# Latent attention loop: two scores by key ahead of the value products, and the fourth score by key of a step moved into the next step

## The chip, the cores and the metric

One core of one Trainium2 chip runs the whole program in one launch. The metric is the device time in microseconds (us). The program is a stack of four layers, each a cross attention and a feed-forward block, over 4 batches of 512 tokens of width 128. The change touches only the loop of the latent attention in the third layer, which takes some 210 us of the 1221 us.

## The reference, cut to what matters

Within the third layer's feed-forward block stands a latent attention (`_mla`): keys and values come from a latent of width 64, there are 16 heads of width 8, and a causal mask.

```python
def _mla(h, Wq, Wdkv, Wuk, Wuv, Wo):
    q = (h @ Wq).reshape(B, S, HEADS, hd)
    c = h @ Wdkv
    k = (c @ Wuk).reshape(B, S, HEADS, hd)
    v = (c @ Wuv).reshape(B, S, HEADS, hd)
    scores = jnp.einsum('bqhd,bkhd->bhqk', q, k) / jnp.sqrt(jnp.asarray(hd, h.dtype))
    causal = jnp.tril(jnp.ones((S, S), bool))
    scores = jnp.where(causal, scores, jnp.asarray(-1000000000.0, h.dtype))
    a = jax.nn.softmax(scores, axis=-1)
    out = jnp.einsum('bhqk,bkhd->bqhd', a, v).reshape(B, S, D)
    return out @ Wo
```

## The kernel before

Every engine runs its own hand-written program; semaphores tie them together. The latent attention is one loop over steps k = -8 to 75 (`STEPS`). A step stands for one head, and there are 64 heads in all (4 batches of 16), in 16 groups of four (a group is n, a head of it g). Each score matrix is made twice:

- `score(step, way)`, L933: scores by query, 512, 384, 256 and 128 columns for way 0 to 3 (causal). VectorE takes the largest of each row (`largest`, L2049). It runs `LEAD` = 8 steps ahead, so step k issues the scores of head k + 8.
- `score_by_key(step, j)`, L945: the transposed scores with the row maximum folded in, 512, 384, 256 and 128 columns for j = 0 to 3. ScalarE takes their exponent out of PSUM (`exponent`, L1309).
- `weigh(n, j)`, L961: eight fp32 matmuls (rows of the trace) with 32 stationary columns, probabilities times values, 512, 384, 256 or 128 columns. It runs `LAG` = 5 steps behind; so the 512-column one falls on k = 1, 5, 9, ..., the 128-column one on k = 4, 8, 12, ....
- `beside(name, n)`, the extras, at most one a step (`extra(k)`): projections of the next batch ("values" L907 at k = 10, 26, 42; "keys" L902 at 12, 28; "queries" L904 at 14, 30), "turn" L912 at every k = 1, 5, 9, ..., which transposes the row maxima of a group, and the way out ("out" L916 at 7, 15, 23, ..., "mix" L919 at 8, 24, 40, 56, "write" L922 at 11, 27, 43, 59). For k below 0 they are "values", "keys" and "queries" of batch 1 and the turn of group 0. They share PSUM bank 7, so each waits until the one before is read.

Scores by query share three PSUM banks, and scores by key three others (`RINGS` = 3), so each of the two kinds waits for the reader of the tile three before:

```python
wait(pe, qk_max, t - RINGS + 1)   # in score
wait(pe, kq_exp, t - RINGS + 1)   # in score_by_key, t = 4 * step + j
```

By this, `score_by_key(k, 3)` waits for the exponent of `(k, 0)`, `(k, 0)` for that of `(k - 1, 1)`, `(k, 1)` for that of `(k - 1, 2)` and `(k, 2)` for that of `(k - 1, 3)`. The probabilities have two sets of buffers (by n % 2). So on ScalarE the first exponent of a group carries one more wait, for a value product:

```python
if g == 0 and j == 0:
    wait(act, pv_ps, n - 1)
```

The value products of group n - 2 end with the one at step k = 4n, so that wait is for the `weigh` of the very step in which the exponent stands.

GpSimd masks the diagonal of each head's probabilities (`hide_later_keys`, L1534, waits for all four exponents of the head; `weigh` waits for it), splits the maxima of a group in pieces (`split_max`, L1512 to L1518, ahead of its turn) and, after ScalarE has copied the turn (L1298), spreads the result into the queries (`spread`, L1527), for which `score_by_key(4n, 0)` waits. SyncE brings the operands of each group by 18 DMAs (`stack`, L497); those of group n wait until the scores by key of group n - 4 are all done, and are first used by `score(4n, 0)`, at step 4n - 8. After groups 3, 7 and 11 it also spills the next batch (L486), and the next group's loads wait for the spill.

Of the kernel before, what the change touches and what calls it, by code (L numbers as in the profile page):

```python
# [20 lines left out]
TB = S // P  # L21
# [73 lines left out]
def extra(k):  # L95

    for name, every, offset, first, count in (("keys", 16, -20, 1, B), ("queries", 16, -18, 1, B), ("values", 16, -6, 0, B),
                                              ("turn", 4, -3, 0, QUADS), ("out", 8, 15, 0, UNITS),
                                              ("mix", 16, 24, 0, B), ("write", 16, 27, 0, B)):
        n, rest = divmod(k - offset, every)  # L100
        if rest == 0 and first <= n < count:
            return name, n
    return None
# [76 lines left out]
def build(nc, x_in, packed, w_ffn1, w_moe, w_mla, split2, w_ffn3, rope, mask1, mask3, normed1, sums1, out):  # L180
    ctx = ExitStack()
    with ctx:
# [341 lines left out]
        def _(pe):  # L524
# [366 lines left out]
            def beside(name, n):  # L891


                if (name, n) != EXTRAS[0]:
                    last = EXTRAS[NTH[name, n] - 1]
                    pe.wait_ge(extra_read, read(*last))
                    if last[0] == "write":
                        pe.wait_ge(x_new, XNEW0[MLA] + last[1] + 1)
                bank = ps[:, 7, :]
                block_of = lambda i: slice(i * P, (i + 1) * P)  # L900
                if name == "keys":
                    t = mm(bank, w_uk, c_s[0:LAT, cols(n)], start=True, stop=True)  # L902
                elif name == "queries":
                    t = mm(bank, w_q, FT[:, cols(n)], start=True, stop=True)  # L904
                elif name == "values":
                    for i in range(TB):
                        t = mm(bank[:, block_of(i)], c_s[0:LAT, n * S + i * P:n * S + (i + 1) * P], w("mwuv", LAT),  # L907
                               start=True, stop=True)
                elif name == "turn":
                    pe.wait_ge(nm_split, n + 1)  # L910
                    for i in range(TB):
                        t = mm(ps[SIGNS:P, 7, block_of(i)], nm_pieces[:, n % 2, i, :], identb[:, :], start=True, stop=True)  # L912
                elif name == "out":
                    pe.wait_ge(oT_sb, n + 1)
                    for i in range(TB):
                        t = pe.transpose(bank[:, block_of(i)], oT[:, block_of(i)], ident)  # L916
                elif name == "mix":
                    for i in range(TB):
                        t = pe.transpose(bank[:, block_of(i)], o_s[:, n * TB + i, :], ident)  # L919
                else:  # L920
                    for i in range(TB):
                        t = mm(bank[:, block_of(i)], oT_s[:, block_of(i)], w("mwo"), start=True, stop=True)  # L922
                t.then_inc(extra_ps, 1)
# [12 lines left out]
            def score_by_key(step, j):  # L936


                n, g = divmod(step, WAYS)
                t = WAYS * step + j  # L940
                if g == 0 and j == 0:
                    pe.wait_ge(neg_set, n + 1)
                wait(pe, kq_exp, t - RINGS + 1)
                rows = SIGNS + PIECES * WAYS
                mm(ps[:, 2 * (t % RINGS) + 1, 0:S - j * P], keys[0:rows, n % HOLD, g, j * P:(j + 1) * P],  # L945
                   queries[0:rows, n % HOLD, g, j * P:S], start=True, stop=True).then_inc(kq_ps, 1)
# [18 lines left out]
                    t.then_inc(pv_ps, 1)  # L965

            for k in STEPS:
                if extra(k) is not None:
                    beside(*extra(k))
                ahead, now = 0 <= k + LEAD < TB * QUADS, 0 <= k < TB * QUADS  # L970
                if ahead:
                    score(k + LEAD, 0)
                    score(k + LEAD, 1)
                if 0 <= k - LAG < TB * QUADS:
                    weigh(*divmod(k - LAG, TB))
                if now:
                    score_by_key(k, 0)
                if ahead:
                    score(k + LEAD, 2)
                if now:  # L980
                    score_by_key(k, 1)
                if ahead:
                    score(k + LEAD, 3)
                if now:
                    score_by_key(k, 2)
                    score_by_key(k, 3)

            prepare(MOE, lambda b: route(MOE, b, w("mgw")))
            pe.wait_ge(ld["moe"], 16)
# [57 lines left out]
        def _(act):  # L1047
# [264 lines left out]
            for k in STEPS:  # L1312
                if k >= 13 and (k - 13) % 8 == 0 and (k - 13) // 8 < UNITS:
                    u = (k - 13) // 8
                    act.wait_ge(pv_ps, 2 * u + 2)
                    if u >= 1:
                        act.wait_ge(extra_ps, put("out", u - 1))
                    go(oT, ps[:, 6, :], ACT.Copy).then_inc(oT_sb, 1)
                if extra(k) is not None:
                    beside(*extra(k))  # L1320
                if 0 <= k < TB * QUADS:
                    for j in range(TB):
                        exponent(k, j)

            starts(act, MOE)
            for b in range(B):
# [975 lines left out]
```

## Time and profile before

| | |
|---|---|
| median of 3 runs | 1234.56 us (1230.53 to 1235.0) |
| the profiled execution | 1222.78 us |
| its span | 1221.0 us |
| mean granted TensorE clock of the span | 0.892 |
| TensorE matmuls busy | 1003.9 us (82%) |
| VectorE, ScalarE, GpSimd busy | 830.3, 519.1, 485.9 us |

The profiled execution was 0.95% faster than the median of the other runs. In a view in order of time, a row has the start in us, the duration in us (of the whole merged run of instructions where "x2" or more stands behind), the engine, the line, the operation, output <- inputs and their size, and in brackets how long the engine sat idle before and what ended that. The durations of matmuls overlap, since they are pipelined: what a matmul costs TensorE is the distance to the start of the next. PE is TensorE, DVE VectorE, ACT ScalarE, POOL GpSimd, SPq SyncE's queue. In a view of busy time by stretch, a row has the stretch, its length, the busy us (and instructions) of matmuls, weight loads, VectorE, ScalarE and GpSimd, the granted clock, the DMA share and GB/s. The granted clock is that of TensorE, 1.00 being the 2.4 GHz level and 0.50 the 1.2 GHz level.

### The profile page before, as it was taken

Reading aid. Unit: us, or ns where it says so; the run is one execution under the profiler, and the core shown is the slowest. Engines: PE = TensorE matmul, PEld = TensorE weight load, DVE = VectorE, ACT = ScalarE, POOL = GpSimd, SP = SyncE. Lnnn points to the kernel's source line nnn. Section 1 sums busy time; section 2 is a strip of 40 time slices with the busy share of each in tenths; the row PEclk is TensorE's granted clock in tenths of the full one; section 3 lists DMA queues with packets and bytes.
Section 4 is the critical chain, followed back from the end, with each engine's and each line's share of the span. In section 5 each row is a group of like instructions: output and inputs, shape, how many; then the busy total and the mean of one; then the engine's idle time right before and its main releaser. Section 6 shows DMA issues by size and latency. Waiting matters only on the chain.

```text
span 1221.0 us, 20581 instructions
## 1 busy us (share of the span) xinstructions
PE 1003.9 (82%) x6807; PEld 720.7 (59%) x6811; DVE 830.3 (68%) x2125; ACT 519.1 (43%) x1266; POOL 485.9 (40%) x433
## 2 busy tenths in 40 slices
PE   4798795677776999967998698888889999569977
PEld 2577633556666899845776233333356777347774
DVE  4599488499966777578998366666423333778972
ACT  2455251244422555653442246665622333135532
POOL 3244254255514666213556666564530000314430
PEclk8899796589977999988999669999977999789998
DMA  8200000000011111220000222221020000000001
GB/s 307 98 1 1 1 1 0 1 1 1 1 36 26 45 42 45 85 74 1 0 1 1 82 67 64 70 77 50 11 87 1 0 0 0 1 1 1 1 1 35
DMA packets 22964, 40.21 MB, mean 33 GB/s; under 512 B 6272, under 2 KB 17792, under 8 KB 22240
## 3 DMA queue, kind: packets, MB, share of 16 engines
q1 hardware_dynamic: 20384, 33.99, 8.6%
q0 software_dynamic: 2496, 5.16, 1.6%
q8 instruction: 46, 0.75, 0.3%
q14 instruction: 38, 0.31, 0.1%
HBM read 31.31 MB, written 7.82 MB: 32 GB/s over the span
## 4 chain that ended last, share of the span: by engine, by line
PE 49%; issue 20%; DVE 15%; POOL 9%; ACT 5%; DMA 1%; SPq 1%; DVEq 0%; POOLq 0%; ACTq 0%
PE ps L800 6%; PE ps L716 5%; PE ps L752 5%; PE ps L742 4%; POOL att L1406 4%; PE ps L961 3%; PE ps L812 3%; DVE mx L1676 3%; PE ps L945 3%; PE ps L933 2%; DVE rs L1690 2%; PE ps L699 2%; PE ps L682 2%; PE ps L534 1%; PE ps L573 1%
## 5 line engine op out<-in xcount | busy, mean ns | idle before, releaser
L1406 POOL TENSOR_TENSOR att<-att,ri 128x1232 f32<-128x1232 f32 x64 | 177.5, 2773 | 221.1 <-DVE ri L1696 221.1
L716 PE MATMUL ps<-VW,PT 128*128 128x128 f32 (+3 forms) x1280 | 159.5, 280 | 29.5 <-DVE x L1708 27.8
L716 PEld LDWEIGHTS ps<-VW,PT 128*128 128x128 f32 (+1 forms) x1280 | 150.0, 193 | 48.8 <-DVE x L1708 44.4
L1139 ACT ACTIVATE PT<-ps 128x512 f32<-128x512 f32 x128 | 69.9, 595 | 129.1 <-PE ps L699 129.1
L2049 DVE CUSTOM_DVE_ANT_0 C<-ps,cmaskb 128x512 bf16<-128x512 f32 (+1 forms) x128 | 71.2, 557 | 70.9 <-PE ps L933 65.9
L1131 ACT ACTIVATE att<-att 128x1232 f32<-128x1232 f32 x64 | 79.0, 1234 | 51.6 <-DVE att L1683 51.5
L699 PE MATMUL ps<-W,att 128*128 128x128 f32 (+1 forms) x640 | 85.0, 282 | 12.0 <-POOL att L1406 12.0
L1690 DVE TENSOR_REDUCE rs<-att 128x16 f32<-128x1232 f32 x64 | 91.2, 1425 | 0.0
L1805 DVE SCALAR_TENSOR_TENSOR U<-ps,w_c,U 128x128 f32 x128 | 36.0, 344 | 77.8 <-PE ps L752 77.8
L752 PEld LDWEIGHTS ps<-U,att 128*128 128x128 f32 x512 | 68.2, 196 | 33.6 <-issue 31.4
L800 PE MATMUL ps<-PT,att 128*128 128x128 f32 x624 | 81.1, 285 | 4.3 <-issue 2.8
L945 PE MATMUL ps<-U,W 108*128 108x512 bf16 (+3 forms) x256 | 71.8, 327 | 15.0 <-ACT VW L1309 5.7
L933 PE MATMUL ps<-W,U 72*128 72x512 bf16 (+3 forms) x256 | 73.6, 337 | 12.7 <-DMA W<-split 8.1
L699 PEld LDWEIGHTS ps<-W,att 128*128 128x128 f32 (+1 forms) x640 | 72.7, 143 | 16.0 <-POOL att L1406 12.6
L800 PEld LDWEIGHTS ps<-PT,att 128*128 128x128 f32 x624 | 76.2, 199 | 7.0 <-issue 3.6
L945 PEld LDWEIGHTS ps<-U,W 108*128 108x128 bf16 x256 | 25.6, 102 | 78.5 <-issue 28.9
L752 PE MATMUL ps<-U,att 128*128 128x128 f32 x512 | 69.2, 281 | 2.5 <-ACT att L1168 2.5
L1373 POOL TENSOR_TENSOR rstd<-ve,minus_half 128x4 f32<-128x4 f32 x42 | 42.7, 1032 | 68.2 <-DVE ve L1585 54.7
L1383 POOL TENSOR_TENSOR VBD<-PT,W 128x1232 f32<-128x1232 f32 x6 | 13.5, 2252 | 141.5 <-issue 130.2
L1168 ACT ACTIVATE att<-ps 128x512 f32<-128x512 f32 x64 | 38.1, 597 | 70.5 <-PE ps L742 70.5
L742 PE MATMUL ps<-FT,U 128*128 x128 | 67.6, 616 | 0.0
L1676 DVE TENSOR_REDUCE mx<-ps 128x16 f32<-128x1232 f32 x32 | 46.0, 1438 | 27.8 <-issue 12.3
(332 smaller groups left out, 2225.4 us busy)
## 6 DMA issues: line engine op xcount, KB each, us to landing
U<-in_ffn SPq DMA_DIRECT2D x1, 6176.0 KB, 23.5
U<-split SPq DMA_DIRECT2D x144, 32.0 KB
W<-split SPq DMA_DIRECT2D x144, 32.0 KB
W<-in_packed SPq DMA_DIRECT2D x1, 2162.5 KB, 22.4
U<-in_ffn SPq DMA_DIRECT2D x1, 2060.0 KB, 8.1
U<-in_moe SPq DMA_DIRECT2D x1, 2048.0 KB, 8.4
split<-VBD SPq DMA_DIRECT2D x4, 384.0 KB, 3.0
split<-W SPq DMA_DIRECT2D x4, 384.0 KB, 2.7
```

Of the source, the lines that this page charges most:

```text
L699: q = pe.transpose(ps[0:m, (3 if s == X2 else 4) + k, (c % 4) * P:(c % 4 + 1) * P], att[:, 2 + t.slot(2), c * P:c * P + m], ident)
L716: q = mm(attended(s, t), PT[0:m, t.slot(2), c, :], batch(VW, t.group)[0:m, c * D:(c + 1) * D], start=(c == 0), stop=(c == NC - 1))
L742: mm(ps[:, u % 2, :], W1M[:, e, j * P:(j + 1) * P], FT[:, cols(c)], start=True, stop=True)\
L752: t = mm(ps[:, 4 + e % 2, i * D:(i + 1) * D], hh[:, u % 2, i * P:(i + 1) * P], W2M[:, e, j, :], start=(j == 0 and i == 0), stop=(j == J2 - ...
L800: t = mm(ps[:, 2 + 2 * k + a, c * P:(c + 1) * P], chosen1[:, k, at:at + P], pickedT[:, k, :], start=True, stop=True)
L933: mm(ps[:, 2 * (t % RINGS), 0:(i + 1) * P], queries[0:STACK, n % HOLD, g, i * P:(i + 1) * P], keys[0:STACK, n % HOLD, g, 0:(i + 1) * P], s ...
L945: mm(ps[:, 2 * (t % RINGS) + 1, 0:S - j * P], keys[0:rows, n % HOLD, g, j * P:(j + 1) * P], queries[0:rows, n % HOLD, g, j * P:S], start=T ...
L1131: go(att[:, 2 + t.slot(2), :], att[:, t.slot(2), :], ACT.Exp, scale=scale).then_inc(expd, 1)
L1406: tt(p, p, over_keys(ri[:, t.slot(2), :]), ALU.mult).then_inc(probs, 1)
L1676: v.tensor_reduce(top, src, AX.X, ALU.max).then_inc(rowmax, 1)
L1690: v.tensor_reduce(rs[:, t.slot(2), :], heads(att[:, 2 + t.slot(2), :]), AX.X, ALU.add)\
L2049: v.tensor_tensor_reduce(unused[t % 2][:, 0:z], ps[:, 2 * (t % RINGS), 0:z], visible[:, S - z:S], -1.0, -NEG, ALU.add, ALU.min, nm[:, n % ...
```

## The change

On TensorE the order within a step changes. Before: extra, score 0 and 1, value product, key score 0, score 2, key score 1, score 3, key scores 2 and 3. After: score 0 and 1, key score 3 of the step before, score 2, key scores 0 and 1, value product, extra, score 3, key score 2. On ScalarE the extra moves from ahead of the four exponents to between the second and the third. VectorE, GpSimd and SyncE keep their order. No instruction is added or taken out.

```diff
@@ TensorE
             for k in STEPS:
-                if extra(k) is not None:
-                    beside(*extra(k))
                 ahead, now = 0 <= k + LEAD < TB * QUADS, 0 <= k < TB * QUADS
                 if ahead:
                     score(k + LEAD, 0)
                     score(k + LEAD, 1)
-                if 0 <= k - LAG < TB * QUADS:
-                    weigh(*divmod(k - LAG, TB))
-                if now:
-                    score_by_key(k, 0)
+                if 0 <= k - 1 < TB * QUADS:
+                    score_by_key(k - 1, TB - 1)
                 if ahead:
                     score(k + LEAD, 2)
                 if now:
+                    score_by_key(k, 0)
                     score_by_key(k, 1)
+                if 0 <= k - LAG < TB * QUADS:
+                    weigh(*divmod(k - LAG, TB))
+                if extra(k) is not None:
+                    beside(*extra(k))
                 if ahead:
                     score(k + LEAD, 3)
                 if now:
                     score_by_key(k, 2)
-                    score_by_key(k, 3)
@@ ScalarE
-                if extra(k) is not None:
-                    beside(*extra(k))
-                if 0 <= k < TB * QUADS:
-                    for j in range(TB):
-                        exponent(k, j)
+                now = 0 <= k < TB * QUADS
+                if now:
+                    exponent(k, 0)
+                    exponent(k, 1)
+                if extra(k) is not None:
+                    beside(*extra(k))
+                if now:
+                    exponent(k, 2)
+                    exponent(k, 3)
```

On TensorE, step k = 9 in the kernel before: the turn (L912), scores by query (L933), the 512-column value product (L961) and the key scores (L945).

```order
L912 MATMUL ps<-identb,VBD 32x128 x4
L933 MATMUL ps<-W,U 128x512
L933 MATMUL ps<-W,U 128x384
L961 MATMUL ps<-VW,KBD 32x512
L961 MATMUL ps<-KBD 32x512 x2
L961 MATMUL ps<-PT,KBD 32x512
L945 MATMUL ps<-U,W 128x512
L933 MATMUL ps<-W,U 128x256
L945 MATMUL ps<-U,W 128x384
L933 MATMUL ps<-W,U 128x128
L945 MATMUL ps<-U,W 128x256
L945 MATMUL ps<-U,W 128x128
```

The same step on TensorE in the changed kernel.

```order
L933 MATMUL ps<-W,U 128x512
L933 MATMUL ps<-W,U 128x384
L945 MATMUL ps<-U,W 128x128
L933 MATMUL ps<-W,U 128x256
L945 MATMUL ps<-U,W 128x512
L945 MATMUL ps<-U,W 128x384
L961 MATMUL ps<-VW,KBD 32x512
L961 MATMUL ps<-KBD 32x512 x2
L961 MATMUL ps<-PT,KBD 32x512
L912 MATMUL ps<-identb,VBD 32x128 x4
L933 MATMUL ps<-W,U 128x128
L945 MATMUL ps<-U,W 128x256
```

The 128-column key score that closed the step now comes third, and is that of head 8; the value product has gone from third place to behind key score 1, and the turn from the top to behind it.

On ScalarE, steps k = 9 and 10 before: the turn's copy (L1298), the exponents (L1309) and the copies of "values" (L1294).

```order
L1298 ACTIVATE VBD<-ps 12x512
L1309 ACTIVATE att<-ps 128x512
L1309 ACTIVATE att<-ps 128x384
L1309 ACTIVATE att<-ps 128x256
L1309 ACTIVATE att<-ps 128x128
L1294 ACTIVATE att<-ps 128x8x8 x8
L1309 ACTIVATE VW<-ps 128x512
L1309 ACTIVATE VW<-ps 128x384
L1309 ACTIVATE VW<-ps 128x256
L1309 ACTIVATE VW<-ps 128x128
```

The same two steps on ScalarE in the changed kernel.

```order
L1309 ACTIVATE att<-ps 128x512
L1309 ACTIVATE att<-ps 128x384
L1298 ACTIVATE VBD<-ps 12x512
L1309 ACTIVATE att<-ps 128x256
L1309 ACTIVATE att<-ps 128x128
L1309 ACTIVATE VW<-ps 128x512
L1309 ACTIVATE VW<-ps 128x384
L1294 ACTIVATE att<-ps 128x8x8 x8
L1309 ACTIVATE VW<-ps 128x256
L1309 ACTIVATE VW<-ps 128x128
```

The third and fourth exponents of a step with an extra now stand behind the extra's copy.

## Rows read from the trace of the kernel before

**Rows 1.** Busy time and granted clock in three stretches of the loop

```profile
712.00:724.00 12.00, 12.00 (x50) 5.39 (x48) 8.66 (x40) 8.26 (x22) 8.47 (x16) 0.50 0.17 51
740.00:760.00 20.00, 17.07 (x127) 6.50 (x125) 13.14 (x58) 12.85 (x33) 15.66 (x25) 1.00 0.17 47
880.00:905.00 25.00, 18.36 (x125) 7.90 (x122) 4.97 (x21) 8.81 (x23) 4.52 (x7) 0.70 0.00 0
```

**Rows 2.** TensorE in order of time, start of steps 13 and 29

```profile
746.56 0.55 PE L933 MATMUL ps<-W,U 72*128 72x512 bf16 x2
...
794.24 0.55 PE L933 MATMUL ps<-W,U 72*128 72x512 bf16 x2
```

**Rows 3.** TensorE in order of time, step 22, which has no extra

```profile
771.74 0.54 PE L933 MATMUL ps<-W,U 72*128 72x512 bf16 x2
772.21 0.52 PE L961 MATMUL ps<-att 128*32 128x384 f32 x2
...
772.99 0.39 PE L945 MATMUL ps<-U,W 108*128 108x512 bf16 x1
773.22 0.27 PE L933 MATMUL ps<-W,U 72*128 72x256 bf16 x1
773.33 0.33 PE L945 MATMUL ps<-U,W 108*128 108x384 bf16 x1
773.50 0.22 PE L933 MATMUL ps<-W,U 72*128 72x128 bf16 x1
773.56 0.27 PE L945 MATMUL ps<-U,W 108*128 108x256 bf16 x1
774.07 0.23 PE L945 MATMUL ps<-U,W 108*128 108x128 bf16 x1 [0.24 <-ACT KBD L1309]
```

**Rows 4.** ScalarE in order of time, the four exponents of step 22

```profile
773.42 1.43 ACT L1309 ACTIVATE KBD<-ps 128x512 f32<-128x512 f32 x4 [0.98 <-PE ps L945]
```

**Rows 5.** VectorE in order of time, step 28, whose four tiles follow one another

```profile
789.92 0.68 DVE L2066 TENSOR_TENSOR U<-U,ps 128x512 f32<-128x512 f32 x1
...
792.30 0.69 DVE L2049 CUSTOM_DVE_ANT_0 C<-ps,cmaskb 128x512 bf16<-128x512 f32 x1
...
793.95 0.08 DVE L2049 DVE_READ_ACCUMULATOR2_ANT VBD<- 128x1 f32 x1
```

**Rows 6.** TensorE, two steps whose extra waits for VectorE: mix, keys

```profile
777.65 0.66 PE L919 MATMUL ps<-W,C 128*128 128x128 f32 x4 [0.66 <-DVE C L2061]
...
790.75 1.09 PE L902 MATMUL ps<-C,U 64*128 64x512 f32 x2 [0.62 <-DVE U L2066]
```

**Rows 7.** An extra on TensorE and its copy on ScalarE: turn, values

```profile
757.69 0.40 PE L912 MATMUL ps<-identb,VBD 128*32 128x128 bf16 x4
...
758.33 0.59 ACT L1298 ACTIVATE VBD<-ps 12x512 bf16<-12x512 f32 x1
...
738.44 1.05 ACT L1294 ACTIVATE att<-ps 128x64 f32<-128x64 f32 x8 [0.58 <-PE ps L907]
```

**Rows 8.** TensorE in order of time ahead of step 0: an extra, two steps

```profile
694.68 2.07 PE L907 MATMUL ps<-W,C 64*128 64x128 f32 x8
696.69 1.14 PE L933 MATMUL ps<-W,U 72*128 72x512 bf16 x3
...
698.57 1.14 PE L933 MATMUL ps<-W,U 72*128 72x512 bf16 x3 [0.19 <-DVE VBD L2049]
```

**Rows 9.** SyncE's queue: loads of groups 7 and 8, with a spill between

```profile
755.73 2.98 SPq L497 DMA_DIRECT2D U<-split  x9
...
767.05 3.26 SPq L497 DMA_DIRECT2D U<-split  x9
770.36 3.36 SPq L497 DMA_DIRECT2D W<-split  x9
```

**Rows 10.** GpSimd, the spread of group 3 after the turn of step 9

```profile
738.62 1.89 POOL L1527 COPY U<-VBD 12x2048 bf16<-12x2048 bf16 x1
```

**Rows 11.** TensorE at step 44, where it waits for VectorE

```profile
840.73 0.23 PE L933 MATMUL ps<-W,U 72*128 72x128 bf16 x1 [1.57 <-DVE VBD L2049]
```

## Prediction

> **What bounds the loop now.** I read busy time by stretch first: from 740 to 760 us, TensorE is busy 17.07 of 20 us, VectorE 13.14, ScalarE 12.85, GpSimd 15.66 [rows 1]. TensorE is nearest to full but idles 15%. The clock is at its 2.4 GHz level there, at 1.2 GHz from 712 to 724, and mixed (0.70) from 880 to 905 [rows 1]. Then the order of time: step 13 starts at 746.56, step 29 at 794.24, so 16 steps take 47.68 us [rows 2], 2.98 each.
>
> A plain step shows where the idle time sits [rows 3]. Start to start: score 0 and 1 with the lead-in of the value product 0.47 us, the 384-column value product 0.78, key score 0 0.23, score 2 0.11, key score 1 0.17, score 3 0.06, key score 2 0.51, then key score 3, and about 0.07 to the next step. Score 2, as wide as key score 2, costs 0.11; so 0.40 of the 0.51 is a wait, and the bracket names ScalarE's exponent. It is the ring of three banks: key score 3 needs the exponent of key score 0, issued only 1.08 us before. That exponent starts 0.43 after its matmul (772.99 to 773.42) [rows 3, 4], runs 0.60, and 0.04 later key score 3 goes. Only VectorE, at step 44 (1.57 us), and two kinds of extra show longer waits of this sort [rows 6, 11].
>
> **What the change removes.** All instructions stay, so only waits and clock can move. Key score 3 now comes behind the next step's score 0 and 1, past a value product and key score 2; its wait goes, if no other takes its place. Bare order of a step after: 0.23 + 0.17 + 0.06 + 0.11 + 0.23 + 0.17 + 0.10 lead-in (0.47 less 0.23 and 0.14 to 0.17 for the two scores) + W + 0.06 + 0.11 = 1.24 + W, W being the value product (0.78 here, and by columns 1.00, 0.57 and 0.36: a quarter is 0.21). Before it is 0.47 + W + 1.08 + 0.07 = 1.62 + W. That is 0.38 a step; the first five steps, at half clock, are full (12.00 of 12.00 us) [rows 1] and have none of it, and the last three, at half clock too, hardly any: 56 x 0.38 = 21.3 us.
> The mix at the top of a step waited for VectorE to read the "out" before it, 0.66 idle; 0.79 us against a normal 0.10 start to start [rows 6]. Now both stand late in their steps, a step apart, and VectorE has time: 3 times (steps 24, 40, 56), 2.4 us. "Keys" of step 28 waited 0.62 for "write" [rows 6]: 0.7 us, once.
> Ahead of step 0 an extra stands between two steps' scores, and VectorE starves: a step with "values" takes 2.01 + 1.88 us (694.68 to 698.57) against 1.88 without [rows 8]. With the extra between score 2 and 3, VectorE reads three tiles beneath it. A step is then about 1.0 (three scores at half clock) + 2.0, say 3.1 instead of 3.9: near 0.7 x 3 = 2 us. Sum of what goes: 26.4 us.
>
> **What it adds.** (a) The first exponent of a group waits for the value product of its own step. That product stood before key score 0, and now stands behind key score 1. Walk step 4n from its start: key score 0 at 0.57, key score 1 at 0.80, value product (128 columns) 1.07 to 1.43, its result seen about 0.15 later (a 512-column result is seen 0.43 after a start whose issue is 0.23: an estimate) [rows 3, 4]. So exponent 0 starts at 1.58, not 1.00; exponents 1 and 2 at 2.07 and 2.45 (four of them fill 1.43 us) [rows 4]. TensorE is at key score 3 at 2.00 and gets its bank at 2.23; at key score 0 at 2.40, bank at 2.60; at key score 1 at 2.83, bank at 2.88. Together 0.48 us, for steps 8 to 60: 14 x 0.48 = 6.7 us. No row shows this wait before; its bounds are nothing (covered by a later wait on the value product) and 1.0 (the whole 0.58 shift twice).
> (b) ScalarE's copy now stands ahead of exponents 2 and 3, and key score 1 of the next step needs exponent 2. Turn at T: copy starts T + 0.64, lasts 0.59 [rows 7], exponent 2 takes some 0.4 more: T + 1.6. TensorE is there at T + 0.33 + 0.97 = T + 1.3. So 0.3 us, 14 times: 4.2. The same sum for "values" (TensorE through in 1.0, copy seen 1.2 after its start and 1.05 long [rows 7]) gives 0.6, 3 times; keys, queries and mix 0.25 to 0.3, together 8 times. (b) is 8.2 us.
> (c) Score 3 is issued behind value product and extra. VectorE needs 1.73 us for four tiles [rows 5]; a late score 3 leaves score 0 and 1 of the next step waiting, 0.1 to 0.4, in about 8 steps. Step 28's "write" keeps VectorE for 2.38 us (789.92 to 792.30) [rows 5]; this was beneath the keys' wait, and now costs TensorE about 0.9. Together 2.5 us. Step 44's 1.57 us stays.
> GpSimd's waits (value product of step 17 and 33 behind the split) and those for ScalarE's copy of the finished product once in 8 steps stay as they are.
> Added: 6.7 + 8.2 + 2.5 = 17.4. Net 26.4 - 17.4 = 9 us. The profiled execution would go from 1222.8 to 1213.8; the median of the runs shown is 0.95% above it, and on that scale I forecast 1234.6 - 9 = 1225.5 us.
>
> **A rule and the clock.** From 712 to 724 TensorE is busy without a gap, bf16 scores alone, and the granted clock stays 0.50 [rows 1]. The Trainium skill (TensorE: Matmul & The Clock Gate, "What's actually happening") has sustained matmul activity release the throttle. By that rule the denser stretch ahead of step 0 would lift the clock sooner; the row speaks against it, and the sum leaves it out.
>
> **Rivals.**
> Nothing new waits: 26.4 us go, and SyncE's loads become the limit. Loads of group 7 start at 755.73, those of group 8 are issued until 773.72 [rows 9], and TensorE wants them at about 778.1, behind the mix at 777.65. With some 2 us of landing (estimate) 2 us are spare. Eight steps that lose 3.8 us would wait about 2 us, at steps 24 and 40. So 26.4 - 4 = 22 us: 1212. It needs (a) and (b) to be hidden; I see nothing that hides them. 0.10.
> The clock rises early: the stretch from 712 (step 0 to 4, some 2.3 us a step) runs at 2.4 GHz down to VectorE's 1.73. 5 x 0.6 = 3 us more: 1222.5. The full 12 us at 0.50 speak against it. 0.05.
> The waits change places: each 0.1 us more in the ring a step costs 6 us, and 0.15 more eats the gain; the range -3 to +3, 1234. For it: three rings are coupled and every cover in (a) to (c) is under 0.6 us. Against it: the 0.40 goes from each step, the new waits from less than half. 0.20.
> Slower: the turn's chain. Before, the spread of group 3 ends at 740.5 [rows 10], and key score 0 of step 12 comes 1.7 us ahead of step 13's 746.56: 4.4 us spare. Now the turn is 2.1 us later in its step (0.57 + 0.40 + 0.10 + 1.00), three steps are together 1.1 shorter, key score 0 is 0.3 earlier in its own, and GpSimd must first mask with an exponent some 0.4 later. That leaves 0.5. If the chain is x later than that, each of 15 groups loses x: from x = 1.0 on, 15 us eat the 9 and pass +0.5%. At x = 1.1: 1242. Against it: 1.6 us of error in a chain of rows is much. 0.07.
> A lower clock at new stalls (TensorE sits 1.57 us idle in step 44 [rows 11]; the clock is 0.70 at the end, where it has little to do): a further 3 us stretch at 1.2 GHz costs 1.5 us. It would widen my case, and is in its range.
>
> **How the numbers follow.** The likeliest case (0.58) is 9 us less, with its own range of 4 to 15 (bounds of (a) 0 to 14, (b) and (c) by half, the clock by 3). A measurement of this kernel tells 0.5%, 6 us, from no change. Faster by more: 0.52 of 0.58, and the first two rivals, 0.67. Slower by more: the turn's chain and what lies beyond, 0.10. Same: 0.23. The range leaves out most of the first rival and the slower one: 1214 to 1233.
>
> **What would show it.** Right: key score 3 without its 0.24 idle; 16 steps (13 to 29) in about 45.5 us; waits of key scores 0 and 1 for ScalarE in steps 4n + 1 and after extras; mix without a wait; the step with "values" ahead of step 0 at 3.1 us. Wrong: a row in which key score 0 waits for GpSimd's spread; score 0 waiting for DMA; score 3 waiting for VectorE in most steps; a clock under 1.00 between 724 and 840. Outside the loop nothing should change.

## The result, and the profile after

The changed kernel takes 1215.4 us (median of four runs, 1212.0 to 1218.2) against 1233.6 of the kernel before beside it: a ratio of 0.9875, 95% interval 0.9841 to 0.9909, so 15.4 us less (11 to 20). The forecast was 9 us less, 1225.5. Its profiled execution took 1215.4 us, span 1213.6.

Below, the loop runs from the first score by query (L933) to the first instruction of the next stage on TensorE (L534): 213.05 us before, 197.6 after, 15.45 less. Behind it both need 316 to 317 us. Ahead of it the executions of all kernels here differ by up to 18 us, because the stretch in which GpSimd issues its 78 gathers and scatters, which none of the edits touches, takes between 124.5 and 138.0 us; so traces are compared by their loops, and times by ratios taken beside the kernel before. "Step k" starts with score 0 of that step. In the changed kernel VectorE's `largest` is L2053 and GpSimd's mask L1538; the lines of TensorE and ScalarE are as before.

Busy time by stretch, changed kernel: steps -8 to -1, 712 to 724 and 740 to 760 us, steps 13 to 28, 29 to 44, 45 to 54, 55 to key score 0 of step 63, and the whole loop.

```profile
699.69:718.48 18.79, 16.68 (x48) 6.41 (x49) 13.72 (x61) 2.83 (x11) 11.30 (x19) 0.50 0.33 97
712.00:724.00 12.00, 11.46 (x41) 4.53 (x39) 9.23 (x43) 4.93 (x11) 10.48 (x14) 0.50 0.25 78
740.00:760.00 20.00, 18.90 (x139) 8.11 (x138) 12.99 (x58) 14.52 (x43) 14.10 (x19) 1.00 0.19 55
750.14:797.00 46.86, 42.28 (x307) 17.85 (x304) 31.70 (x142) 30.80 (x83) 29.16 (x46) 0.93 0.24 71
797.00:841.67 44.67, 40.11 (x302) 17.27 (x303) 31.88 (x144) 29.47 (x81) 27.89 (x43) 0.96 0.24 72
841.67:866.24 24.57, 23.64 (x177) 9.31 (x177) 18.78 (x84) 17.86 (x45) 12.48 (x21) 0.93 0.14 39
866.24:884.46 18.22, 15.28 (x123) 6.34 (x121) 5.07 (x23) 13.19 (x35) 9.50 (x14) 1.00 0.00 1
699.69:897.28 197.59, 177.64 (x1212) 75.56 (x1213) 126.98 (x563) 119.46 (x322) 112.16 (x178) 0.87 0.19 58
```

The same view of the kernel before, of the same steps (-8 to -1, 13 to 28, 29 to 44, 45 to 54, 55 to key score 0 of 63, the loop).

```profile
691.08:711.52 20.44, 17.38 (x48) 6.43 (x49) 13.45 (x61) 2.83 (x11) 13.18 (x20) 0.50 0.36 102
...
746.56:794.24 47.68, 40.85 (x306) 16.88 (x305) 32.19 (x143) 28.99 (x83) 28.70 (x45) 1.00 0.24 69
794.24:841.39 47.15, 39.68 (x305) 16.50 (x303) 31.88 (x140) 28.51 (x82) 26.99 (x43) 1.00 0.24 67
841.39:868.78 27.39, 24.57 (x179) 9.19 (x177) 19.09 (x86) 17.11 (x47) 13.58 (x21) 0.94 0.13 35
868.78:892.31 23.53, 19.02 (x130) 6.73 (x128) 5.55 (x23) 13.29 (x37) 9.07 (x15) 0.81 0.00 1
...
691.08:904.14 213.06, 181.94 (x1213) 73.19 (x1214) 127.23 (x563) 115.23 (x322) 112.71 (x178) 0.88 0.19 53
```

From 740 to 760 us TensorE is busy 18.90 of 20 us, against 17.07 [rows 1]. The gain by stretch: 1.65 us ahead of step 0, 0.9 in steps 0 to 4, 2.5 in 5 to 12, 0.8 in 13 to 28, 2.5 in 29 to 44, 2.8 in 45 to 54, 5.3 in the tail; the drain behind key score 0 of step 63 is 1.0 longer. Over the loop the mean granted clock hardly moved (0.88, 0.87), but its places did: in steps 13 to 28 it fell from 1.00 to 0.93, in the tail it rose from 0.81 to 1.00.

What TensorE's matmuls waited for in the kernel before, from step 0 to 880 us (us in total, times, longest). The view adds up idle brackets.

```profile
PE ps L945 <- ACT VW L1309: 4.8, 18, 0.4
PE ps L945 <- ACT att L1309: 4.0, 14, 0.5
PE ps L945 <- ACT KBD L1309: 3.2, 13, 0.2
PE ps L933 <- DVE VBD L2049: 1.8, 2, 1.6
PE ps L961 <- POOL PT L1534: 1.8, 2, 0.9
PE ps L945 <- ACT PT L1309: 1.7, 7, 0.2
```

The same view of the changed kernel, with ScalarE's waits for a value product (L961), which before had no row.

```profile
PE ps L933 <- DVE VBD L2053: 4.4, 7, 2.0
ACT att L1309 <- PE ps L961: 4.3, 7, 0.6
ACT VW L1309 <- PE ps L961: 3.7, 6, 0.6
PE ps L961 <- POOL PT L1538: 2.4, 2, 1.5
PE ps L945 <- ACT att L1309: 1.1, 3, 0.6
PE ps L945 <- ACT VW L1309: 1.0, 3, 0.4
PE ps L945 <- ACT KBD L1309: 0.5, 2, 0.2
PE ps L945 <- ACT PT L1309: 0.2, 1, 0.2
```

By this view key scores waited for exponents 52 times, 13.7 us, and now 9 times, 2.8 us; scores by query now wait 4.4 us for VectorE, against 1.8. ScalarE does wait for the value product, as term (a) said.

The brackets undercount, in both kernels. A bracket starts at the modelled end of the matmul before, and short ones aren't shown: in step 22 the bracket of key score 3 is 0.24 us, but it starts 0.51 behind key score 2, where 0.11 is usual, so 0.40 is lost [rows 3]. I therefore also count from start to start: the distance of a matmul to the one before it, less what the same pair takes where nothing waits, in steps 5 to 54, without the stretches at half clock, where the granted clock is 0.50 (137.8 us of the kernel before, 116.6 of the changed one). So counted, the key scores waited for exponents 48 times, 19.8 us, and now 28 times, 6.0 us; the scores by query waited 1.9 us for VectorE and now 8.1 us, in 27 waits. This is the count that the sum of the prediction has to be held against.

TensorE in order of time, changed kernel: the step with "values" ahead of step 0; step 17, whose value product waits for GpSimd; steps 19 and 20; steps 28 and 44, whose score 3 waits for VectorE.

```profile
703.55 1.14 PE L933 MATMUL ps<-W,U 72*128 72x512 bf16 x3 [0.19 <-DVE VBD L2053]
704.62 2.07 PE L907 MATMUL ps<-W,C 64*128 64x128 f32 x8
...
764.12 1.06 PE L961 MATMUL ps<-VW,KBD 128*32 128x512 f32 x1 [1.51 <-POOL PT L1538]
...
770.26 0.54 PE L933 MATMUL ps<-W,U 72*128 72x512 bf16 x2
770.64 0.22 PE L945 MATMUL ps<-U,W 108*128 108x128 bf16 x1
...
772.05 0.54 PE L933 MATMUL ps<-W,U 72*128 72x512 bf16 x2
...
773.80 0.68 PE L933 MATMUL ps<-W,U 72*128 72x512 bf16 x2
...
796.52 0.23 PE L933 MATMUL ps<-W,U 72*128 72x128 bf16 x1 [0.93 <-DVE VBD L2053]
...
841.19 0.23 PE L933 MATMUL ps<-W,U 72*128 72x128 bf16 x1 [1.98 <-DVE VBD L2053]
841.67 0.93 PE L933 MATMUL ps<-W,U 72*128 72x512 bf16 x2
842.39 0.31 PE L945 MATMUL ps<-U,W 108*128 108x128 bf16 x1
```

Two waits without a bracket, changed kernel: from key score 2 of step 36 to score 0 and 1 of step 37, and key scores 0 and 1 of step 38, which stands behind a turn, and of step 39, which doesn't.

```profile
818.20 0.27 PE L945 MATMUL ps<-U,W 108*128 108x256 bf16 x1
818.48 0.68 PE L933 MATMUL ps<-W,U 72*128 72x512 bf16 x2
...
822.25 0.75 PE L945 MATMUL ps<-U,W 108*128 108x512 bf16 x2
...
824.45 0.54 PE L945 MATMUL ps<-U,W 108*128 108x512 bf16 x2
```

Score 0 of step 37 starts 0.28 behind key score 2, where 0.11 is usual: 0.17 of waiting for VectorE. Key scores 0 and 1 take 0.21 longer behind the turn: key score 1 waits 0.20 for its exponent.

Step 19 (256-column value product) takes 1.79 us and step 20 (128 columns) 1.75; the bare order of the prediction gave 1.24 + 0.57 = 1.81 and 1.24 + 0.36 = 1.60. Key score 3, now behind score 1, has no bracket any more [rows 3]. At step 45 score 0 and key score 3 start 0.72 us apart (841.67 to 842.39) where step 19 has 0.38 (770.26 to 770.64): behind the 1.98 us of idle time the granted clock is 0.50 (841.7 to 845.1 us).

### The profile page after: what moved, and what is told of

Its sections match the earlier page's. It is cut to its first block, busy times and chain, and to the rows that moved or that the text cites. A ratio compares the mean times of both kernels' runs of the same rounds, so it can differ in the third digit from the quotient of the medians.

```text
span 1213.6 us, 20585 instructions
## 1 busy us (share of the span) xinstructions
PE 1001.9 (83%) x6811; PEld 722.2 (60%) x6811; DVE 830.8 (68%) x2125; ACT 521.4 (43%) x1266; POOL 484.7 (40%) x433
## 4 chain that ended last, share of the span: by engine, by line
PE 49%; issue 20%; DVE 15%; POOL 10%; ACT 3%; DMA 1%; SPq 0%; DVEq 0%; POOLq 0%; ACTq 0%
PE ps L800 6%; PE ps L752 5%; POOL att L1410 5%; PE ps L742 4%; PE ps L716 4%; PE ps L961 4%; PE ps L933 3%; PE ps L812 3%; PE ps L945 3%; DVE mx L1680 2%; DVE rs L1694 2%; PE ps L534 2%; PE ps L598 1%; DVE stats L1577 1%; PE ps L699 1%
## 5 line engine op out<-in xcount | busy, mean ns | idle before, releaser
L800 PE MATMUL ps<-PT,att 128*128 128x128 f32 x624 | 79.4, 282 | 10.2 <-issue 10.2
L2053 DVE CUSTOM_DVE_ANT_0 C<-ps,cmaskb 128x512 bf16<-128x512 f32 (+1 forms) x128 | 71.1, 555 | 20.0 <-PE ps L933 16.6
L800 PEld LDWEIGHTS ps<-PT,att 128*128 128x128 f32 x624 | 74.8, 196 | 13.7 <-issue 13.3
L2053 DVE CUSTOM_DVE_ANT_0 U<-ps,cmaskb 128x384 bf16<-128x384 f32 (+1 forms) x128 | 53.9, 421 | 41.2 <-PE ps L933 41.2
L933 PE MATMUL ps<-W,U 72*128 72x512 bf16 (+3 forms) x256 | 68.7, 345 | 15.8 <-DMA W<-split 9.0
L699 PEld LDWEIGHTS ps<-W,att 128*128 128x128 f32 (+1 forms) x640 | 72.2, 142 | 14.3 <-POOL att L1410 11.0
L945 PE MATMUL ps<-U,W 108*128 108x512 bf16 (+3 forms) x256 | 72.7, 324 | 4.9 <-ACT VW L1309 2.1
```

The source lines that it names most:

```text
L699: q = pe.transpose(ps[0:m, (3 if s == X2 else 4) + k, (c % 4) * P:(c % 4 + 1) * P], att[:, 2 + t.slot(2), c * P:c * P + m], ident)
L800: t = mm(ps[:, 2 + 2 * k + a, c * P:(c + 1) * P], chosen1[:, k, at:at + P], pickedT[:, k, :], start=True, stop=True)
L933: mm(ps[:, 2 * (t % RINGS), 0:(i + 1) * P], queries[0:STACK, n % HOLD, g, i * P:(i + 1) * P], keys[0:STACK, n % HOLD, g, 0:(i + 1) * P], s ...
L2053: v.tensor_tensor_reduce(unused[t % 2][:, 0:z], ps[:, 2 * (t % RINGS), 0:z], visible[:, S - z:S], -1.0, -NEG, ALU.add, ALU.min, nm[:, n % ...
```

## The experiments

There are twelve runs. Each was taken on one of several chips, beside the kernel before on that chip. One table for all; "half" is the time of the loop in which the trace records TensorE's clock at 0.50, and the last column is the loop brought to 50 us of it, at 0.35 us for each us. This price is an estimate from two executions of one kernel (below). It isn't the same everywhere (about 0.2 in the tail, by the fill below), so differences of 1 us in this column say little.

| kernel | ratio (95%) | loop, us | half, us | at equal clock |
|---|---|---|---|---|
| before | | 213.05 | 52.6 | 212.1 |
| before, profiled again | | 213.06 | 52.6 | 212.2 |
| key score 3 moved alone | 0.9986 (0.9970 to 1.0002) | 204.1 | 50.5 | 203.9 |
| the same, again | 0.9998 (0.9982 to 1.0014) | 209.57 | 66.2 | 203.9 |
| extras moved alone | 0.9928 (0.9904 to 0.9951) | 207.84 | 60.5 | 204.2 |
| key scores 0, 1 ahead alone | 0.9882 (0.9848 to 0.9915) | 198.32 | 55.0 | 196.6 |
| both moves, extras at the top | 0.9899 (0.9870 to 0.9927) | 199.16 | 55.9 | 197.1 |
| **changed kernel** | 0.9875 (0.9841 to 0.9909) | 197.6 | 50.8 | 197.3 |
| it, copies behind all exponents | 0.9873 (0.9853 to 0.9893) | 199.6 | 52.8 | 198.6 |
| it, value product first in steps 4n | 0.9859 (0.9813 to 0.9904) | 194.01 | 40.4 | 197.4 |
| it, extra behind score 2 | 0.9847 (0.9823 to 0.9872) | 194.26 | 50.9 | 193.9 |
| the last two together | 0.9798 (0.9765 to 0.9832) | 193.14 | 49.8 | 193.2 |
| before, tail filled | 1.0013 (0.9994 to 1.0031) | 215.41 | 51.6 | 214.9 |
| changed, tail filled | 0.9878 (0.9841 to 0.9915) | 199.29 | 49.0 | 199.6 |

### The change in parts

Key score 3 alone, all else as before.

```diff
                 if ahead:
                     score(k + LEAD, 0)
                     score(k + LEAD, 1)
+                if 0 <= k - 1 < TB * QUADS:
+                    score_by_key(k - 1, TB - 1)
                 if 0 <= k - LAG < TB * QUADS:
                     weigh(*divmod(k - LAG, TB))
...
-                    score_by_key(k, 3)
```

> The kernel before with one part of the change alone: key score 3 goes behind the next step's scores 0 and 1; extras stay at the top of a step, the value product stays ahead of key score 0. The loop (first score by query to the first warm-up matmul of the next stage) took 213.0 us before and 197.6 after. Theory of the coupled rings: the 0.38 us wait goes, but key score 0 still follows the value product, so exponents start late and the new waits are of nearly the same size; loop 204 to 207, 16 plain steps some 1.4 us shorter. Rival (the fourth key score's move is the gain, the rest is decoration): loop 197 to 200.

Measured: a loop of 204.1 us, within the 204 to 207 expected, but a ratio of 0.9986. The same kernel was run once more.

> The kernel with key score 3 alone moved, once more: its first profile showed a loop of 204.1 us, 9.0 less than before, but its median over 10 runs only 0.14% (1.7 us) less. If the loop is the same in every execution, the profile gives 203.5 to 204.7 again and the ratio of times should come nearer to 0.993 (9 us). The rival: the loop itself varies from execution to execution by where TensorE's clock falls, and the first profile caught a good one; then the loop comes out at 206 to 212 or the ratio stays at 0.997 to 1.000.

Busy time by stretch of its first profile: steps 13 to 28, 29 to 44, the loop.

```profile
755.50:802.64 47.14, 40.17 (x307) 17.79 (x305) 32.19 (x146) 29.64 (x82) 28.54 (x45) 0.96 0.23 68
802.64:849.70 47.06, 39.31 (x304) 17.49 (x303) 32.08 (x144) 29.82 (x83) 28.24 (x44) 0.96 0.25 72
...
702.55:906.65 204.10, 175.48 (x1213) 75.35 (x1213) 127.23 (x563) 117.70 (x322) 112.28 (x178) 0.88 0.19 56
```

The same of its second profile.

```profile
743.98:793.09 49.11, 42.15 (x306) 18.20 (x304) 32.61 (x147) 30.44 (x84) 29.22 (x46) 0.91 0.23 67
793.09:843.55 50.46, 42.83 (x304) 18.01 (x303) 32.27 (x143) 29.33 (x81) 27.43 (x43) 0.87 0.23 67
...
691.45:901.02 209.57, 181.10 (x1213) 76.25 (x1213) 127.33 (x563) 117.81 (x322) 112.33 (x178) 0.84 0.19 54
```

The instructions are the same, and so is the tail (19.40 us in both); the 5.5 us lie where the clock is lower, 15.7 us more of it at 0.50 in all: 0.35 us for each. So the rival holds: the loop of this kernel varies with the clock. No key score waits for an exponent in either profile, and still its time is that of the kernel before over 22 runs. At equal clock the profiles give 8 us less. The record of the runs shows where these went: each run has its granted clock, averaged over the whole span. It averages 0.888 and 0.887 in the two sets of this kernel, against 0.894 in both sets of the kernel before beside them, which is 15 and 17 us more at half clock. At 0.35 us each, the kernel is 8.1 and 6.3 us faster at equal clock; at 0.23 us (the slope of time against half-clock time among runs of one kernel on one chip, over all 125 recorded runs of this kind) 6.3 and 4.3. So moving key score 3 alone does remove time, and most of it is lost again to a lower clock. In which part of the program the clock is lower the averages don't tell; in the two profiles it is the loop.

The kernel before didn't vary so in its two profiles:

> The kernel before, profiled once more, to see how much its loop of 213.05 us varies from one execution to another. If the loop is fixed by its program, it gives 212.5 to 213.6; if half-clock stretches come and go, up to 3 us either way, with the step lengths differing only in those stretches. The part ahead of the loop (691.1 us in the first profile, 699.7 to 709 in those of the other kernels) shows how much of the spans is not the loop's doing.

Busy time by stretch, its whole loop in the second profile.

```profile
692.78:905.84 213.06, 181.95 (x1213) 73.20 (x1214) 127.25 (x563) 115.22 (x322) 112.47 (x178) 0.88 0.18 53
```

213.06 us, within the 212.5 to 213.6 expected, and stage by stage within 0.01 us of the first. Ahead of the loop it took 692.8 us, 691.1 the first time.

The extras moved alone, on TensorE and ScalarE as in the change.

```diff
-                if extra(k) is not None:
-                    beside(*extra(k))
...
                     score_by_key(k, 1)
+                if extra(k) is not None:
+                    beside(*extra(k))
                 if ahead:
                     score(k + LEAD, 3)
```

> The kernel before with only the extras moved: on TensorE to between key score 1 and score 3, on ScalarE to between exponents 1 and 2; the value product and the four key scores stay. It has the gains at mix, keys and ahead of step 0, but keeps the wait of key score 3. Ring theory: 1.6 us ahead of step 0, 3 us at mix and keys, and at steps with an extra the wait of key score 3 shrinks, since the extra now stands between key score 0 and it: loop 203 to 207 (213.0 before). Rival (late copies cost as much as in term b): 210 or more.

Measured 207.84 us, just above the 203 to 207 expected, with 8 us more at half clock than the kernel before; ratio 0.9928. Ahead of step 0 it takes 18.80 us like the changed kernel (20.44 before).

Key scores 0 and 1 ahead of the value product alone; extras at the top, key score 3 at the end of its step.

```diff
-                if 0 <= k - LAG < TB * QUADS:
-                    weigh(*divmod(k - LAG, TB))
-                if now:
-                    score_by_key(k, 0)
                 if ahead:
                     score(k + LEAD, 2)
                 if now:
+                    score_by_key(k, 0)
                     score_by_key(k, 1)
+                if 0 <= k - LAG < TB * QUADS:
+                    weigh(*divmod(k - LAG, TB))
```

> The kernel before with the other part alone: score 2, key scores 0 and 1 ahead of the value product, then score 3, key scores 2 and 3; extras at the top, key score 3 in its own step. Theory of the coupled rings: the value product (0.36 to 1.00 us) now stands between key score 0 and key score 3 and hides the exponent; no wait at key score 3 but behind the 128-column product: loop 192 to 196, as good as with the fourth moved. Rival (the fourth key score must leave the step): its wait stays in most steps, loop 204 or more.

What TensorE's key scores waited for there, from step 0 to 884 us.

```profile
PE ps L945 <- ACT VW L1311: 2.1, 5, 0.4
PE ps L945 <- ACT att L1311: 1.8, 4, 0.5
```

198.32 us, above the 192 to 196 expected, but at a ratio of 0.9882: nearly all of the gain, without moving key score 3 at all. Between key score 0 and key score 3 there now stands a value product, and the exponent of key score 0 runs beneath it: 9 waits, 3.9 us by this view, against 52 and 13.7. So this half of the change removes the same wait as the other half, and the two don't add.

Both moves with the extras at the top: the changed kernel with this taken back on TensorE and ScalarE.

```diff
             for k in STEPS:
+                if extra(k) is not None:
+                    beside(*extra(k))
...
                     weigh(*divmod(k - LAG, TB))
-                if extra(k) is not None:
-                    beside(*extra(k))
```

> The changed kernel with the extras back at the top of a step, on TensorE and on ScalarE. Theory of the coupled rings: the late copies cost 0.3 to 0.6 us each (term b) and the late score 3 some more (c), so without them the loop is shorter by 4 to 5 us in spite of the waits for mix and keys and of the 1.6 us ahead of step 0 that come back: loop 192 to 195. Rival (late extras are part of the gain, since they remove the waits for mix, keys and the starved steps): loop 199 to 202.

199.16 us, the rival's 199 to 202, ratio 0.9899; but 197.1 at equal clock against 197.3 of the changed kernel. Taken by themselves the extras are worth 8 us; with the key scores ahead, nothing that the loops show at equal clock.

### The terms (a) and (b)

Value product first in every fourth step, so that exponent 0 of a group needn't wait for it.

```diff
                     score(k + LEAD, 1)
+                if k % TB == 0 and 0 <= k - LAG < TB * QUADS:
+                    weigh(*divmod(k - LAG, TB))
...
-                if 0 <= k - LAG < TB * QUADS:
+                if k % TB != 0 and 0 <= k - LAG < TB * QUADS:
                     weigh(*divmod(k - LAG, TB))
```

> The changed kernel, but in steps k = 0, 4, 8, ... the value product stands ahead of score 2 and of the key scores, so exponent 0 of a group no longer waits for it. Term (a) of the prediction puts that wait at 0.48 us in 14 steps, 6.7 us: loop 190 to 192. Rival (it is covered by the wait for VectorE's ring right behind it): loop 196 to 198.

ScalarE's waits for L961 are gone, but TensorE's for exponents hardly fell (2.8 to 1.9 us by brackets; 6.0 to 5.7 from start to start, steps 5 to 54). Steps 9, 21, 37 and 53, each behind the first of a group, shrink by 0.04 us (2.76 to 2.72, 3.20 to 3.16). In the tail, where no score by query is left to wait for VectorE, the wait is bare: from key score 0 of step 56 to that of 57 it takes 1.52 us and not 2.38, the same from 60 to 61; part of it is lost again a step earlier, and the tail takes 17.41 us and not 18.22, both at 1.00. The loop is 194.01 us, between the two expectations, with 10.4 us less at half clock; at equal clock it is 197.4, no less than the changed kernel. So term (a) is worth some 0.5 us in the steps and 0.8 in the tail, not 6.7: the rival was right up to the tail, and the shorter loop is the clock's.

ScalarE's copies of the extras behind all four exponents, TensorE as in the change.

```diff
                     exponent(k, 0)
                     exponent(k, 1)
-                if extra(k) is not None:
-                    beside(*extra(k))
...
                     exponent(k, 2)
                     exponent(k, 3)
+                if extra(k) is not None:
+                    beside(*extra(k))
```

> The changed kernel with one edit on ScalarE: the extra's copy stands behind all four exponents. TensorE as changed. Term (b) of the prediction says that the copy between exponents 1 and 2 costs 0.3 to 0.6 us each at the next key score 1, 8.2 us in all. If so, the loop falls from 197.6 to 189 to 192. Rival (the rings of VectorE and ScalarE hide each other, so one of them freed gives little): 195 to 197.

199.6 us (198.6 at equal clock), above both expectations, ratio 0.9873. Its waits over steps 13 to 28:

```profile
PE ps L961 <- POOL PT L1536: 2.6, 1, 2.6
PE ps L933 <- DVE VBD L2051: 1.2, 2, 0.9
PE ps L961 <- ACT U L1320: 1.1, 1, 1.1
```

The key scores have no bracket here; from start to start they waited 1.5 us in steps 5 to 54, not 6.0. So (b) was there, and 4.5 us of it go, but nothing is won: from step 0 to 873 us, by brackets, the value products now wait 4.6 us for GpSimd's mask (2.4 in the changed kernel) and 2.4 us for ScalarE's copy of the product before (0.3). That the later copies hold GpSimd up is my reading of the mask's wait at step 17 (2.6 us, 1.5 in the changed kernel); no run shows it apart.

The extra behind score 2, ahead of key score 0, its copy ahead of the exponents.

```diff
                     score(k + LEAD, 2)
+                if extra(k) is not None:
+                    beside(*extra(k))
                 if now:
                     score_by_key(k, 0)
...
-                if extra(k) is not None:
-                    beside(*extra(k))
```

> The changed kernel with the extra between score 2 and key score 0 on TensorE and ahead of the four exponents on ScalarE. Theory of the coupled rings: it keeps what the late extras gave (VectorE busy beneath them ahead of step 0, no wait at mix and keys) and takes the copy out from between the exponents: loop 188 to 192, some 6 to 9 us shorter than the changed kernel's 197.6. Rival (an extra this early meets VectorE or ScalarE late and waits): loop 196 to 200.

194.26 us, ratio 0.9847, 3.3 us less than the changed kernel with the same 51 us at half clock. That is less than expected (188 to 192); the three mixes wait for VectorE again, 1.7 us. Its steps 13 to 28, and the loop:

```profile
757.06:799.48 42.42, 39.38 (x306) 16.34 (x304) 31.85 (x142) 31.64 (x83) 29.23 (x46) 1.00 0.27 78
...
706.02:900.28 194.26, 177.04 (x1212) 72.73 (x1213) 127.46 (x563) 122.81 (x322) 112.60 (x178) 0.87 0.20 59
```

Here the extra and its copy pass before key score 0 wants an exponent, and GpSimd gets what it waits for earlier (1.7 us of waits for its mask, 2.4 in the changed kernel).

This with the value product first in steps 4n:

> The kernel with the extra behind score 2 (194.3 us of loop), and in every fourth step also the value product ahead of key score 0, so that the first exponent of a group doesn't wait for it. If the wait of term (a) costs what it was sized at (0.48 us a group), the loop falls by 5 to 7 us, to 187 to 189. The rival: the product first in the changed kernel hardly altered its step lengths (0.04 us a group), so that wait is mostly covered by the ring; then the loop is 193 to 195, within 1.5 us, and the ratio to the kernel before stays at 0.984 to 0.986. Another half-clock stretch in or out adds or takes 2 to 3 us.

193.14 us, the shortest of all: 1.1 us less, of which the clock accounts for 0.4. The rival again, by its loop. Its ratio of 0.9798 lies below the rival's 0.984 to 0.986, and is 0.5% lower than that of the kernel without. The record of the runs gives this to the clock: it averages 0.896 over its six runs against 0.892 in the kernel before beside them (14 us less at half clock), and 0.893 against 0.894 in the kernel without (2 us less). At 0.35 us each the two are 18.5 and 18.1 us faster than the kernel before, at 0.23 they are 20.1 and 18.3, each good to about 2: no gain of (a)'s 6.7 in it. TensorE there waits for a load of SyncE once in steps 13 to 28, 0.2 us.

### The tail

Unused scores by query (`fill`) in the last eight steps of the kernel before, where it has none of its own. They have the same widths, the other two stand in the places of score 2 and 3, and their results aren't read.

```diff
                 if ahead:
                     score(k + LEAD, 0)
                     score(k + LEAD, 1)
+                elif now:
+                    fill(0)
+                    fill(1)
```

> The kernel before, with four unused scores by query (same sizes, no reader) issued in each of steps 56 to 63, which have no scores ahead of their own; work is added, none is taken away. In the profile of before these steps take 23.5 us (step 55 to key score 0 of step 63) and the granted clock falls to 0.50 from 883.4 to 893.6 us; in the changed kernel they take 18.2 us at 1.00. Clock theory (most of the 5.3 us there is the clock): with TensorE kept busy the clock stays at 1.00 and the steps take 19 to 21 us although 0.5 us of matmuls is added to each. Ring theory (the 5.3 us are waits on the exponents): the steps stay at 23 us or grow, whatever the clock does.

The same in the changed kernel.

> The changed kernel with unused scores (same widths) in the last eight steps, where it has none of its own, so that TensorE stays busy there. If the gain in the tail (18.2 us from step 55 to key score 0 of step 63, against 23.5 before) came from TensorE's clock, the fill takes nothing from it and the filled kernels before and after stand equal, at 23 to 24. If it came from the ring (key score 3 waiting for its own step's first exponent before), the filled one keeps it: 18 to 20 against 23.5 of the kernel before with the same fill. The drain behind it keeps 11.8 to 12.8 unless the clock falls later, then 0.5 to 1 less.

Steps 55 to key score 0 of step 63 in the kernel before, filled.

```profile
882.49:906.01 23.52, 20.09 (x160) 8.36 (x158) 5.55 (x23) 13.32 (x37) 9.06 (x15) 1.00 0.00 1
```

The same in the changed kernel, filled.

```profile
864.43:884.31 19.88, 18.78 (x155) 8.70 (x152) 5.09 (x23) 14.19 (x36) 9.50 (x14) 1.00 0.00 1
```

Both at clock 1.00 and with the same work, the new order is 3.6 us shorter, so the ring's part of the gain in the tail is shown. The fill costs 1.7 us at that clock (19.88 against 18.22 in the changed kernel). In the kernel before it changes nothing (23.52 filled at 1.00, 23.53 unfilled at 0.81). So of the 5.3 us in the tail 3.6 are the ring's and 1.7 the clock's, if the fill costs both kernels the same, which isn't shown.

## Why the prediction was right, and where it was off

**The wait that goes: right, by place and by size.** Key score 3 has no idle time any more. From start to start it had waited 0.39 to 0.46 us in each of 48 steps, 19.8 us in all, where the prediction took away 0.38 a step; the bare steps take 1.79 and 1.75 us where 1.81 and 1.60 were worked out. But the prediction gave this gain to key score 3's move; the run with two key scores ahead alone shows that the other half removes most of it as well.

**Ahead of step 0: right.** The step with "values" takes 3.16 us (3.1 was forecast), the stretch 1.65 us less (2 forecast).

**The mix and the keys: right.** Neither has an idle bracket. What step 28 lost instead is the 0.93 us of score 3 behind "write" (0.9 forecast).

**Term (a): near nothing up to the tail.** It stood at 0.48 us in 14 steps, 6.7 us. The walk through step 4n has TensorE arrive on time at every key score. It doesn't: in nearly every step 4n + 1 score 0 and 1 have just waited 0.30 to 0.43 us for VectorE, and taking the value product out of the way gains 0.04 us. In the tail, where no score by query waits, it gains 0.8 us for two groups, near the 0.48 of each. The prediction had named this bound ("covered by a later wait"), but for the wait on the value product and not for VectorE's.

**Term (b): the mechanism right, the size somewhat too large.** Key score 1 waits 0.20 us behind each turn (0.3 forecast), 0.51 behind "values" (0.6), 0.29 behind "keys", 0.40 behind "queries" and 0.17 behind the mix (0.25 to 0.3). In steps 5 to 54 at full clock these are 20 waits and 5.4 us of the 6.0, where the forecast for the same 20 gives 6.8; the other 0.6 are key scores 0 and 1 in steps 9, 21, 37 and 53.

**Term (c): too small.** From start to start VectorE's waits grew from 1.9 to 8.1 us, 6.1 more, where 2.5 were forecast for (c). By brackets alone it looks right (1.8 to 4.4). Step 28 was foreseen, 1.0 us. Score 0 and 1 together wait 0.30 to 0.43 us in 11 steps 4n + 1, which the forecast had as 0.1 to 0.4 in about 8, and score 3 waits 0.38 in steps 16, 32 and 48, where it had 0.07. That step 44 "stays" at 1.57 was wrong by 0.4: it is 1.98.

**The tail: not seen.** It gained 5.3 us. The prediction had 0.38 for each of its steps to 60, near 2.3, and expected nothing of the clock.

**The clock: its risk was priced, but left out of the sum.** "16 steps (13 to 29) in about 45.5 us" came out at 46.86, because the clock fell to 0.93 behind the wait of step 17; 6.8 us at half clock cost 2.4 us at the price above, and 44.5 would be left. The prediction said that "a further 3 us stretch at 1.2 GHz costs 1.5 us"; at 0.35 us each it is 1.1. It also named "a clock under 1.00 between 724 and 840" as a sign of being wrong. That sign was badly set: the kernel before is itself at 0.50 until 726.3. In the changed kernel the clock is at 0.50 until 732.5, from 763.2 to 770.0 and from 797.3 to 800.7, and the forecast held all the same.

**How the sum comes out, and the luck in it.** An estimate from these counts: (a), (b) and what else reaches a key score cost 6.0 us in steps 5 to 54 and not 14.9, (c) 6.1 and not 2.5, so 12.1 in place of 17.4. That would give 26.4 - 12.1 = 14.3. The tail adds 3.0 beyond its share, and steps 0 to 4, for which nothing was forecast, 0.9. The 10.2 us more at half clock in steps 5 to 54 take 3.6, the longer drain 1.0 and step 17's longer wait for GpSimd 0.6. That leaves 13.0 of the 15.45 found; 56 steps at 0.41 in place of 0.38 are another 1.7, and the rest is within what such an account can tell. It leaves out what (a) to (c) cost at half clock and in the tail. So the wait that goes, and the kinds of waits that come, were right. That 1215.4 lies in the range of 1214 to 1233, near its lower edge, is in part luck: (a) and (b) were too large by some 7 to 9 us, (c) too small by 3.6, and the tail's surplus and the clock's cost, which the sum both left out, nearly cancelled.

**The rule on the clock.** It was right that the dense stretch from 712 us stays at 0.50: in the changed kernel TensorE was busy 14.00 of 14.00 us from 718.5 to 732.5 at 0.50, and then the clock rose. With the extra behind score 2 it rose at 724.0, stayed up for 3.4 us in which TensorE was busy 2.54, and fell again for 13.7 us in which it was busy 13.19. The clock rose for 30 us or more 32.8 us into the loop in the changed kernel, 35.2 in the one before, and 39.1 with two key scores ahead alone. The Trainium skill (TensorE: Matmul & The Clock Gate, "What's actually happening") has activity release the throttle; no run here speaks clearly for or against it.

**The rivals.** Loads of SyncE never became the limit in the changed kernel, and barely (0.2 us once) in the fastest one. The clock didn't rise early: steps 0 to 4 ran at 0.50. No key score waits for the spread of the turn. The waits did change places in part, from ScalarE's ring to VectorE's: 13.8 us went (19.8 to 6.0), 6.1 came.

## What to carry to other kernels

Count waits from start to start, not by idle brackets: here the brackets showed 2.8 us of 6.0 and 13.7 of more than 19.8, and made a term look right that was too small by more than half. When several rings couple three engines, a new wait that falls behind another engine's is covered by it (0.04 us in place of 0.48) and is bare where that engine has nothing to do. Ask of each half of a reordering whether it removes the same wait by itself. A reordering that leaves gaps of 1 to 2 us behind can cost as much through TensorE's clock as through the gaps. So profile a promising order twice before reading a difference of 5 us, and compare the granted clock of all runs, not of the profiled one alone.

## What was unexpected of the hardware

One and the same kernel, with key score 3 moved alone, had 10.2 us at half clock between the first lasting rise and the tail in one execution and 27.3 us in the other, in four stretches of 6.8 us in place of three of 3.4, for the most part behind the same waits; the loop took 204.1 and 209.6 us. The kernel before, profiled twice, repeated its loop to 0.01 us and each rise and fall of its clock in it. In the changed kernel the stretches begin within or just behind idle times of 1 to 2 us (1.51 us for GpSimd at step 17, 0.93 and 1.98 for VectorE at steps 28 and 44).
